# A gated two-layer kernel on TensorE: a new order of the first group's loads and matmuls, and eight copies moved from VectorE to ScalarE

## What is computed

```python
W, b = L0_W[itok_B_0_63], L0_b[itok_B_0_63]          # one 512x512 matrix and one row per item
y = x + einsum('bsd,bdh->bsh', x, W) + b[:, None, :]  # layer 0
h = gelu(einsum('bnd,hd->bnh', y, fc1_w) + fc1_b)     # fc1: 512 -> 2048, shared by all items
shared = einsum('bnh,sh->bns', h, fc2_w) + fc2_b      # 384 columns, shared
own = einsum('bnh,bph->bnp', h, experts_w[itok_B_0_15]) + experts_b[itok_B_0_15][:, None, :]
out = y + concatenate([shared, own], axis=-1)         # 384 shared and 128 expert columns
```

## Time and profile before

| what | value |
|---|---|
| median of 3 runs | 1615.3 us (1612.68 to 1615.56) |
| the profiled execution | 1612.14 us |
| its span in the profile | 1610.3 us |
| TensorE busy in the span | 99% |
| VectorE, ScalarE busy | 82%, 34% |
| granted TensorE clock, mean over the span | 0.996 |

### The profile page before, as it was taken

One profiled execution on the slowest core, in us unless ns is written; L12 is line 12 of the kernel. 1 busy time (PEld: TensorE's weight loads), 2 busy tenths in 40 slices (PEclk: granted clock), 3 DMA queues, 4 the chain that ended last, 5 costly groups with the idle time before them and its releaser, 6 DMA issues.

```text
span 1610.3 us, 28028 instructions
## 1 busy us (share of the span) xinstructions
PE 1598.0 (99%) x7096; PEld 1322.2 (82%) x7096; DVE 1316.1 (82%) x2192; ACT 555.0 (34%) x926; POOL 13.1 (1%) x17
## 2 busy tenths in 40 slices
PE   7999999999999999999999999999999999999999
PEld 6888888888888888888888888888888888888887
DVE  5988879788788888888888887887888888887865
ACT  4443333333333333333333333333333333333321
POOL 3000000000000000000000000000000000000000
PEclk8999999999999999999999999999999999999999
DMA  7765555555455555555555554555555545555410
GB/s 233 206 180 161 156 152 163 146 155 155 133 169 156 151 153 152 152 157 157 143 157 151 156 163 138 160 148 142 168 155 154 144 139 171 159 155 140 137 53 27
DMA packets 302335, 243.55 MB, mean 151 GB/s; under 512 B 34060, under 2 KB 234892, under 8 KB 302228
## 3 DMA queue, kind: packets, MB, share of 16 engines
q1 hardware_dynamic: 254180, 203.23, 44.5%
q10 hardware_dynamic: 48048, 39.35, 7.8%
HBM read 209.94 MB, written 32.51 MB: 151 GB/s over the span
## 4 chain that ended last, share of the span: by engine, by line
PE 98%; DVE 1%; DMA 0%; ACT 0%; issue 0%; DVEq 0%; POOL 0%; POOLq 0%
PE ps_out L910 43%; PE ps_h L878 22%; PE ps_e L878 22%; PE ps_y L870 11%; PE ps_t L819 1%; DMA e_blocks<-in_L_cond_fc_w 0%; PE ps_h L870 0%; PE ps_h L918 0%; PE ps_out L819 0%; DVE w2e L642 0%; DVE e_whole L705 0%; DVE resid L736 0%; PE ps_e L819 0%; ACT g_raw L560 0%; DVE h L642 0%
## 5 line engine op out<-in xcount | busy, mean ns | idle before, releaser
L910 PE MATMUL ps_out<-w2e,h 128*128 128x512 f32 x3072 | 736.6, 389 | 0.1
L910 PEld LDWEIGHTS ps_out<-w2e,h 128*128 128x128 f32 x3072 | 575.9, 188 | 119.4 <-DVE h L642 0.3
L878 PE MATMUL ps_h<-y_t,w 128*128 128x512 f32 (+1 forms) x1548 | 370.3, 388 | 0.0
L878 PE MATMUL ps_e<-y_t,w 128*128 128x512 f32 (+1 forms) x1548 | 370.3, 388 | 0.0
L878 PEld LDWEIGHTS ps_e<-y_t,w 128*128 128x128 f32 x1548 | 289.6, 188 | 59.5
L878 PEld LDWEIGHTS ps_h<-y_t,w 128*128 128x128 f32 x1548 | 289.3, 188 | 59.3
L546 ACT CAST w2e<-e_whole 128x512 fp32r<-128x512 f32 x256 | 158.7, 620 | 348.2 <-DVE e_whole L705 345.3
L705 DVE STREAM_TRANSPOSE e_whole<-e_blocks 128x512 f32<-128x512 f32 x256 | 277.1, 1082 | 0.0
L724 DVE CAST h<-g_raw 128x512 fp32r<-128x512 f32 x256 | 108.8, 425 | 162.5 <-ACT g_raw L560 158.6
L514 ACT CAST w_split<-w_raw 128x512 fp32r<-128x512 f32 x244 | 144.8, 620 | 190.6 <-DMA w_raw<-in_L_cond_W 96.2
L642 DVE TENSOR_TENSOR w2e<-e_whole,w2e 128x512 fp32r<-128x512 f32 x256 | 175.4, 685 | 18.1 <-ACT w2e L546 18.1
(11 more groups left out here) (76 smaller groups left out, 437.2 us busy)
## 6 DMA issues: line engine op xcount, KB each, us to landing
e_blocks<-in_L_cond_experts_w SPq DMA_DIRECT2D x1024, 64.0 KB, 2.5
w_raw<-in_L_cond_W SPq DMA_DIRECT2D x244, 256.0 KB, 3.9
out<-resid SPq DMA_DIRECT2D x64, 256.0 KB, 2.2
x_blocks<-in_x SPq DMA_DIRECT2D x240, 64.0 KB, 2.4
b_all<-in_L_cond_b SPq DMA_DIRECT2D x60, 256.0 KB, 4.2
x_raw<-in_x SPq DMA_DIRECT2D x60, 256.0 KB, 4.8
y_rows<-y ACTq DMA_DIRECT2D x60, 256.0 KB, 3.9
x_blocks<-y_rows ACTq DMA_DIRECT2D x240, 64.0 KB, 2.7
```

The costliest lines, as they stand in the source:

```text
L878: last = nc.tensor.matmul(h_bank(c)[:, at * S:end * S], w1[:, w, k, c * P:(c + 1) * P], y_t[:, a, k, at:end, :].rearrange("p b s -> p (b s)"),
L910: last = nc.tensor.matmul(ps_out[b][:, :], h[:, c % 2, a, b * S:(b + 1) * S], fc2_columns(c, c % 2, w, b), start=(c == 0 and n == 0), stop ...
```

## The change

The change does five things.

1. SP's loads come in another order. Each of the 16 layer-0 slices is a load of its own (before, from slice 4 on, two in one). SP loads slices 0 and 1, then reads the three other categories and loads all four bias rows, then slices 2 to 15 with x of items 2 and 3, the fc tiles and the experts' weights between them. Fc tiles 0 to 7 are now all loaded by SP; before, ScalarE issued them.
2. The first six fc tiles have a buffer each (other tensors that are free then), so that experts' weights can land in `e_blocks` without waiting for tiles 0 to 3.
3. TensorE's opening: 26 `keep_busy` matmuls in place of 6, at three places, no fc tile ahead of layer 0, tile 0 in its middle, tile 1 at its end, tiles 2 to 4 among `fc1_ahead`, and tiles 5 and 6 inside step 0. The lists of ScalarE and VectorE follow.
4. The four pairs of GpSimd instructions for the bias rows become one pair on 8 rows, with a selecting matrix (`row_of`) in place of ones.
5. In steps 1 to 8 of group 0 `copy_last` is done by ScalarE, behind `e_high` and ahead of `gelu`.

```diff
+        OWN_PREP = 6
+        ACT_COPIES = 8
...
             sp.wait_ge(cats_in, 16)
-            for n, slices in enumerate(FIRST_W):
...
+            first_cats = [category(0, 0)]
+            load_first_w(0)
+            load_first_w(1)
+            for b in range(GB):
+                if b > 0:
+                    first_cats.append(category(0, b))
+                load_b0_row(b)
+            for j in range(2, 6):
+                load_first_w(j)
+            load_first_x(2)
+            for j in range(6, 9):
+                load_first_w(j)
+            load_prep(sp, 0)
+            load_first_w(9)
+            load_first_w(10)
+            load_first_x(3)
             sp.wait_ge(exps_in, 16)
             first_experts = [index(exps, b, exp_w.shape[0]) for b in range(GB)]
-            load_experts(0, 0, first_experts, range(GB))
+            for j in range(11, NC):
+                load_first_w(j)
+                if j < NC - 1:
+                    load_experts(0, 0, first_experts, [0], [j - 11])
+            for t in range(1, QUAD):
+                load_prep(sp, t)
+                load_experts(0, 0, first_experts, [t])
+            for t in range(QUAD, OWN_PREP + PSLOTS):
+                load_prep(sp, t)
...
+            def copy_last(g, c):
+
+                if not copied_by_act(g, c):
+                    return
+                after(act, fc2_done, (g * NC + c - 1) * GB)
+                if c % 4 == 0:
+                    act.wait_ge(prep_lo, prep_count("fc2", NS - 1, c // 4))
+                nc.scalar.copy(ring[:, c % 2, :, :, 1, :],
+                               w2[:, :, c, SHARED - P:].unsqueeze(2).to_broadcast([P, 2, GB // 2, P]))\
+                    .then_inc(first_last_ready, 1)
...
             pe.wait_ge(ident_ready, 1)
+            keep_busy(12)
+            turn_x(0)
             keep_busy(6)
-            turn_x(0)
-            turn_prep(0)
-            turn_prep(1)
             turn_x(1)
-            turn_prep(2)
-            turn_prep(3)
-            for j in range(6):
+            keep_busy(8)
+            for j in range(5):
                 l0_slice(0, j)
```

More of the change, by code:

```diff
@@ L129, in build @@
         b0_in = sem("b0_in")
-        b0_rows_in = [sem(f"b0_rows_in{b}") for b in range(GB)]
+        b0_rows_in = sem("b0_rows_in")
         be_in = sem("be_in")
@@ L194, in prep_in_step, with copied_by_act @@
             return t if first(g) and c > 0 and t < NPREP else None
+        def copied_by_act(g, c):
+            return first(g) and 1 <= c <= ACT_COPIES
         def prep_count(*tile):
@@ L384, in load_b0 @@
                 after(sp, xb_ready, (G - 1) * GB + b)
+                if first(G - 1) and b == 0:
+                    sp.wait_ge(prep_turned, OWN_PREP)
                 sp.dma_start(b0_all[:, :], l0_b[bass.ds(cat, 1), :].to_broadcast([P, D])).then_inc(b0_in, 16)
@@ L408, in load_experts @@
                 after(sp, e_turned, g * NC + QUAD * (quad - 1))
-                if first(g) and quad == 0:
-                    sp.wait_ge(prep_turned, QUAD)
                 if first(g) and quad == 1:
@@ L506, in w_high @@
                 if first(G):
-                    act.wait_ge(w0_in[[j in slices for slices in FIRST_W].index(True)], 16)
+                    act.wait_ge(w0_in[j], 16)
                 else:
@@ L621, in body @@
                     gelu(g, c)
+                    if first(g) and c == 0:
+                        prep_high(6)
                     for n in range(PREP_RATE):
@@ L754, in _ @@
             w_low(0, 9)
[L755 removed]
             w_low(0, 10)
+            y_low(0, 1)
+            prep_low(0)
             w_low(0, 11)
             x_low(0, 3)
[L759 removed]
+            w_low(0, 12)
             y_sum(0, 2)
[L761 to L762 removed]
+            w_low(0, 13)
+            w_low(0, 14)
             y_low(0, 2)
+            w_low(0, 15)
+            prep_low(1)
+            y_sum(0, 3)
+            y_low(0, 3)
             prep_low(2)
[L765 removed]
             prep_low(3)
+            turn_e(0, 0)
             prep_low(4)
             prep_low(5)
[L769 to L771 removed]
             def body(g, more):
@@ L786, in body @@
                     h_high(g, c)
+                    if first(g) and c == 0:
+                        prep_low(6)
                     prep_low(prep_in_step(g, c, 0))
@@ L858, in l0_slice @@
                 if whole(G, b):
-                    pe.wait_ge(w0_in[[j in slices for slices in FIRST_W].index(True)], 16)
+                    pe.wait_ge(w0_in[j], 16)
                 else:
@@ L902, in fc2 @@
                 after(pe, e_lo, g * NC + c + 1)
-                after(pe, last_ready, g * NC + c + 1)
+                if copied_by_act(g, c):
+                    pe.wait_ge(first_last_ready, c)
+                else:
+                    after(pe, last_ready, g * NC + c + 1 - (0 if first(g) and c == 0 else ACT_COPIES))
                 if first(g) and c % 4 == 0:
@@ L934, in _ @@
             l0_slice(0, 8)
-            turn_prep(4)
+            turn_prep(0)
+            turn_y(1)
             l0_slice(0, 9)
-            turn_y(1)
+            l0_slice(0, 10)
             turn_x(3)
-            for j in range(10, 14):
-                l0_slice(0, j)
+            l0_slice(0, 11)
+            l0_slice(0, 12)
             turn_y(2)
+            l0_slice(0, 13)
             l0_slice(0, 14)
-            turn_prep(5)
             l0_slice(0, 15)
+            turn_prep(1)
             fc1_ahead(0, range(KD // 2))
             turn_y(GB - 1)
+            turn_prep(2)
             fc1_ahead(0, range(KD // 2, KD))
-            turn_prep(6)
+            turn_prep(3)
+            turn_prep(4)
             fc1_ahead(1, range(KD))
@@ L953, in body @@
                     fc1(g, c)
+                    if first(g) and c == 0:
+                        turn_prep(5)
+                        turn_prep(6)
                     turn_prep(prep_in_step(g, c, 0))
```

148 lines of the change are left out of this document (67 added, 81 removed).

## The result

The changed kernel takes 1627.7 us (median of 4 executions, 1625.25 to 1630.47) where the kernel before takes 1615.0 (4 beside it, 1612.68 to 1615.56): a ratio of 1.0082, 95% interval 1.0063 to 1.0101. It is slower, as forecast, but by 12.7 us where 4.4 were forecast, and outside the range. The profiled execution took 1630.47 us with a span of 1628.7; it is the slowest of the four, and it has the lowest mean granted clock, 0.992, where the other three have 0.996 to 0.999.

The account below looks back on a forecast made before the run. It took TensorE's own matmuls as the bound, but for the opening. Walking the lists put fc1 of step 3 about 4.4 us later: 1615.3 + 4.4 = 1619.7 us, range 1613.5 to 1623.0.

Parts of the forecast that it names:

- TensorE before layer 0: Opening: fillers replace the tiles' 4.6 us of DMA waits, so layer 0 starts at 11.3 us, not 13.76.
- Slices 0 to 3: Start of layer 0: slices 2 and 3 just in time, four slices done at 14.6 us, a lead of 4.8.
- The rival that the clock falls: Layer 0: the clock falls to half over 8.6 us, adding 2.4 us, so 1622.1 us; chance 0.17.
- Slices 4 to 15, and from there to step 3: Layer 0 from slice 4: 12.2 us work, 7.9 waits; then 21.3 work, 4.65 waits; step 3's fc1 starts at 60.65.
- The moved copies: Group 0, steps 1 and 2: each copy adds 0.52 us to the chain to gelu; 0.5 us taken.
- The bias rows late: Opening: the last bias row lands late, the whole chain is 1.2 us later, 1620.9 us; no separate chance given.
- GpSimd: Opening: four pairs become one; every subtraction counted at 0.69 us, as if GpSimd cost VectorE nothing.
- Its own signs of being wrong: Layer 0 ending before 32, clock below 1.00 between 20 and 40, or TensorE copy waits in steps 3 to 8.

Follow-up runs that it names:

- The run with fillers: Changed kernel plus filler matmuls that nobody reads in TensorE's waits: 1623.8 us, ratio 1.0052 to the kernel before.
- neighbouring rows: Changed kernel with each bias row's two copies going to partitions 2b and 2b + 1, masks to match: 1620.5 us, ratio 1.0042 to the kernel before.
- ScalarE's list: Changed kernel with ScalarE's casts of y and the first fc tile behind the next slices' casts: 1623.0 us, ratio 1.0037 to the kernel before.
- no copies: Changed kernel with all copies on VectorE again (ACT_COPIES = 0): 1629.4 us, ratio 1.0070 to the kernel before.
- item by item: Changed kernel with bias rows, categories and GpSimd's pairs as before, slices 1 to 3 ahead of the second category: 1620.9 us, ratio 1.0028.
- its own run: Slices cast before y on ScalarE, against the changed kernel, fillers in both: 1619.7 us, ratio 1.0030 to the kernel before.

## Why the prediction was right in direction and wrong in size

- **TensorE before layer 0**: right, 11.11 for 11.3. The eight kernels that share this start had 10.09 to 11.36, by how long the first fillers ran at the low level, so this term wanted a range of its own.
- **Slices 0 to 3: the step that failed.** It had slice 2 issued at 8.1 to 8.5, "three times 0.96 + 0.29" behind the first row. The 0.29 was read from rows of before whose two copies go to neighbouring partitions; the diff shows another destination, `b0_rows[b:2 * GB:GB, :]`, and the price was carried over to it without a bound. It was 0.66, and the read behind it 0.73 for 0.48. The issue came at 10.80. It also counted 2.5 us to landing, the figure of an idle queue; slice 2 took 3.7 (issued at 10.80, cast from 14.47), and slice 3 could be cast 2.3 us behind it (16.79), where 0.7 was counted. "Both are just in time" was said of this step, and a step that is just in time wanted a range. The range had the bias rows late by 1.2 us but never slices 2 and 3.
- **The rival that the clock falls: right in kind, wrong in weight and in length.** It got 0.17 and +2.4 us. The run with fillers puts it at 5.0 or more in the profiled execution. What was mis-sized is how long the half level lasts: the prediction took the 8.6 us of the old opening, and the stretches of the changed kernel shown above come to 2 x (5 x 0.31 + 10 x (0.18 + 0.30 + 0.38 + 0.11)) = 22.5 us between 15 and 60. With the busy share of each of these stretches that is some 9 us of added matmul time, an estimate. So the waits did hide a good part, as the prediction had said (2.8 of its 5.2). Where neighbouring rows wait 0.34, 1.22, 0.22, 0.93 and 1.04 us for slices 12, 14 and 15, y of item 3 and tile 8, the changed kernel waits 0.64 in all, for slice 14. The clearest case is fc2 of step 0, whose twelve matmuls take 4.14 us for 3.01, and yet the way from tile 7 to the landmark takes 13.29 for 13.23, since the wait for tile 8 shrank to nothing.
- **The same rival, as an event of its own**: wrong. The three kernels with a late slice 2 and no fillers (changed, ScalarE's list, no copies) all fell to half right behind that wait of 3.12 to 3.39 us. With slice 2 on time, neighbouring rows kept 1.00, with waits up to 1.70, while item by item fell once, from 22 to 26 us, behind a wait of 1.86. The fall wanted one case with the late slice, and not a chance beside it.
- **Slices 4 to 15, and from there to step 3**: right. At full clock with slice 2 nearly on time (neighbouring rows) the first four slices ended at 15.5, where the row of slice 4 begins (14.6 forecast), slices 4 to 15 took until 36.2 (20.1 us forecast, 20.7 measured), and the way to step 3 took 26.4 us (25.95 forecast). The waits named were there: slice 6 0.98 (1.3), slice 8 0.77 (1.1), slice 10 1.70 (1.95), slice 14 1.22 (1.4), y of item 3 0.93 (1.2), tile 7 1.59 (1.8), tile 8 1.04 (1.2). Each is 0.16 to 0.33 shorter than forecast, in the main since the profile counts from the end of the last matmul's record, and the prediction from where TensorE could take the next; so the profile has 5.6 us of waits of over 0.2 in slices 4 to 15 where 7.9 were forecast, in a stretch of about the same length. The price of the written order, 4.2 us, is shown by its own run.
- **The moved copies**: right. 0.5 was taken; in the old opening the one wait grew by 0.52 and the way to the landmark by 0.36, in the changed one no cost can be told, and VectorE gave nothing back.
- **The bias rows late**: wrong as a rival. The last row was in use at 12.12, 2.1 us after its issue at 10.0.
- **GpSimd**: the prediction took its pairs to cost VectorE nothing. One subtraction of 1.77 us speaks against it, without showing the cause; the sum is hardly touched.
- **Its own signs of being wrong**: one came, a clock below 1.00 between 20 and 40.

The account of the changed kernel's landmark, 71.30 against the forecast 60.65, is then: 62.65 - 60.65 = 2.0 us that neighbouring rows keep too (0.9 of them by the fourth slice), 66.30 - 62.65 = 3.65 for the late supply at full clock, and 71.30 - 66.30 = 5.0 for the clock. It holds for one profiled execution of each kernel; in the medians the last term is 3.9.

## What to carry to other kernels

Read the destination of a moved load, not only its bytes: a few rows scattered over partitions ahead of the first large loads cost this opening 2.4 us in the queue, 8.65 at the landmark of the profiled execution, and 0.4% of the time. Before two single profiles are compared, look at the parts that the edit cannot touch: here the start of layer 0 and the landing of slice 3 moved by up to 1.3 us by themselves. And where a clock column says 1.00, check it against the length of a row. Where a forecast says that an input is just in time, ask what else a miss brings down (here the clock), and price the two together, as one case. Take a second profile of the kernel before when the difference is below one per cent: the first was 1.3 us early at the landmark and free of late waits that others have.
